# The finishing steps of three engines, written into both branches of a graph-network kernel

## What is computed

```
h = relu(layernorm(x))
for l in 1..3:                                    # RGCN, 8 relations, mean per relation
    h = relu(h @ root_l + b_l + sum_r mean_over_edges_of_relation_r((h @ W_l[r])[src], dst))
x = x + h
h = relu(layernorm(x))
h = h + segment_sum(h[src], dst)                  # GIN
h = relu(h @ W1 + b1) @ W2 + b2
h = (h - mean(h, axis=0)) * rsqrt(var(h, axis=0) + 1e-5) * gamma + beta
return x + h
```

## Time and profile before

| | |
|---|---|
| median of three runs | 1638.9 us (1638.22 to 1639.16) |
| the profiled execution's own time | 1638.72 us |
| its span, first to last instruction | 1636.7 us |
| mean granted TensorE clock | 0.669 of full |
| busy: TensorE (PE) | 1195.2 us, 73% |
| busy: GpSimd (POOL) | 1190.5 us, 73% |
| busy: VectorE (DVE) | 868.2 us, 53% |
| busy: ScalarE (ACT) | 643.9 us, 39% |

### The profile page before, as it was taken

How to read it: one execution, slowest core, us unless ns; L and a number is a source line. 1 busy time by engine, 2 the same in 40 slices (tenths; PEclk the granted TensorE clock), 3 DMA queues, 4 the chain that set the end, 5 groups by cost and what they waited for, 6 DMA issues and landing times. The chain is left out here.

```text
span 1636.7 us, 17097 instructions
## 1 busy us (share of the span) xinstructions
PE 1195.2 (73%) x4462; PEld 800.1 (49%) x4486; DVE 868.2 (53%) x3262; ACT 643.9 (39%) x1139; POOL 1190.5 (73%) x1257
## 2 busy tenths in 40 slices
PE   6989675757586878777868787875666666666786
PEld 3466444545455645454535354563544444444553
DVE  5778855555553387777787777742222221222214
ACT  5503200000000498888888888840012121212224
POOL 4777777777777777777777777767777777777770
PEclk9999655555555655657585757655576776767888
DMA  7934343434332322323232323322211221212211
GB/s 227 364 94 121 104 132 91 121 93 119 93 112 68 106 53 68 91 59 98 56 104 52 105 54 104 91 74 52 53 52 53 52 53 52 54 52 54 54 52 42
DMA packets 80864, 144.33 MB, mean 88 GB/s; under 512 B 24720, under 2 KB 38266, under 8 KB 80762
## 3 DMA queue, kind: packets, MB, share of 16 engines
q0 software_dynamic: 39936, 81.87, 19.9%
q1 hardware_dynamic: 40394, 60.67, 10.5%
q10 hardware_dynamic: 432, 0.64, 0.2%
HBM read 100.42 MB, written 42.67 MB: 87 GB/s over the span
## 5 line engine op out<-in xcount | busy, mean ns | idle before, releaser
L1154 POOL DMA_INDIRECT rows<-h_table,idx x1186 | 1125.4, 949 | 367.8 <-issue 367.8
L517 PE MATMUL ps_agg<-sel,rows 128*128 128x64 f32 (+13 forms) x2770 | 723.2, 378 | 401.7 <-DMA rows<-h_table,idx 390.6
L517 PEld LDWEIGHTS ps_agg<-sel,rows 128*128 128x128 f32 x2770 | 611.8, 282 | 696.5 <-DMA rows<-h_table,idx 532.9
L897 DVE TENSOR_SCALAR sel<-iota,early,norm 128x64 f32<-128x64 f32 x1186 | 357.0, 334 | 414.3 <-PE ps_agg L517 412.7
L992 DVE TENSOR_TENSOR early<-ps_a,early 128x300 f32 x416 | 197.9, 476 | 122.8 <-PE ps_a L584 115.6
L782 ACT ACTIVATE scratch<-scratch,ones 128x300 bf16<-128x300 f32 x416 | 222.7, 536 | 46.3 <-PE ps_a L584 39.1
L788 ACT ACTIVATE scratch<-iota,code_lo 128x300 f32<-128x300 f32 x416 | 226.5, 545 | 12.5
L491 PE MATMUL ps_h<-w_all,xT 128*128 128x512 f32 x300 | 196.2, 769 | 4.3 <-ACT stage L693 3.2
L875 DVE TENSOR_SCALAR_CACHE_REDUCE agg_s<-scratch,key_f 128x256 bf16<-128x256 int16 x416 | 192.9, 472 | 10.7 <-DMA scratch<-key_rows 9.4
L584 PE MATMUL ps_a<-scratch 128*128 128x300 bf16 x416 | 170.8, 411 | 1.5 <-DVE early L992 1.2
L981 DVE TENSOR_SCALAR scratch<-iota,code_lo 128x128 bf16<-128x128 f32 x416 | 143.8, 346 | 0.0
(11 more groups left out here) (150 smaller groups left out, 622.4 us busy)
## 6 DMA issues: line engine op xcount, KB each, us to landing
h_table<-stage SPq DMA_DIRECT2D x130, 256.0 KB, 2.4
rows<-h_table,idx POOLq DMA_INDIRECT x1186, 2.5
scratch<-key_rows SPq DMA_DIRECT2D x26, 544.0 KB, 4.1
h_table<-scratch SPq DMA_DIRECT2D x20, 256.0 KB, 6.1
x_rows<-in_x SPq DMA_DIRECT2D x6, 256.0 KB, 6.1
w_all<-in_W SPq DMA_DIRECT2D x3, 512.0 KB, 8.2
x_table<-early SPq DMA_DIRECT2D x6, 256.0 KB, 2.3
out<-early SPq DMA_DIRECT2D x6, 256.0 KB
```

The costliest lines, as they stand in the source:

```text
L517: mm = nc.tensor.matmul(sums_of(L, k)[:, at:at + width], rows[:, G % SLOTS, :], sel[:, G % SELS, in_window:in_window + width], start=False ...
L897: done = nc.vector.tensor_scalar(mine, here, dst, weight, ALU.is_equal, ALU.mult)
L1154: pool.indirect_dma_start(rows[:, slot, :], None, table, bass.IndirectOffsetOnAxis(ap=column, axis=0)).then_inc(landed, 16)
```

## The change

On each of ScalarE, VectorE and TensorE the finishing steps become a function `finish()`, which is called at the end of the fast branch and again at the end of the `Else`. The code behind both branches is gone. What the steps do, their order and their semaphores are the same. SyncE's and GpSimd's programs are as before. Cut to its core (TensorE's part has the same form as ScalarE's):

```diff
         @block.scalar
         def _(act):
+            def finish():
+                act.wait_ge(s_fin, 1)
+                nc.scalar.activation(small[:, 3:4], small[:, 2:3], ACT.Sqrt, bias=vecs[:, 7:8]).then_inc(s_fin_sd, 1)
+                act.wait_ge(s_fin, 5)
+                for q in range(GROUPS):
...
@@ -1266,6 +1277,7 @@
                         out_hid(act, q)
                     if q >= 1:
                         out_z(act, q - 1)
+                finish()
             with act.Else():
...
                     scalar_layer(act, L, False)
-            act.wait_ge(s_fin, 1)
-            nc.scalar.activation(small[:, 3:4], small[:, 2:3], ACT.Sqrt, bias=vecs[:, 7:8]).then_inc(s_fin_sd, 1)
-            act.wait_ge(s_fin, 5)
-            for q in range(GROUPS):
...
+                finish()
 
         @block.vector
         def _(dve):
+            def finish():
+                dve.wait_ge(s_fin_sd, 1)
+                nc.vector.reciprocal(small[:, 4:5], small[:, 3:4]).then_inc(s_fin, 1)
...
@@ -1430,6 +1451,7 @@
                 dve.wait_ge(s_bn, outs)
                 nc.vector.bn_aggr(small[:, 1:3], bn[:, 0:outs, :].rearrange("p b s -> p (b s)")).then_inc(s_fin, 1)
+                finish()
             with dve.Else():
...
                 nc.vector.bn_aggr(small[:, 1:3], bn[:, 0:SUMS[GIN], :].rearrange("p b s -> p (b s)")).then_inc(s_fin, 1)
-            dve.wait_ge(s_fin_sd, 1)
-            nc.vector.reciprocal(small[:, 4:5], small[:, 3:4]).then_inc(s_fin, 1)
...
+                finish()
```

More of the change, by code:

```diff
@@ L1187, in _ @@
         def _(act):
+            def finish():
[3 more added lines that the diff above has]
+                for q in range(GROUPS):
+                    b0, b1 = x_groups[q]
+                    if q >= 2:
+                        act.wait_ge(s_yturn, q - 1)
+                    nc.scalar.activation(y_turn[:, q % 2, 0:P * (b1 - b0)], xT[:, P * b0:P * b1], ACT.Identity,
+                                         bias=small[:, 6:7], scale=small[:, 5:6]).then_inc(s_y, 1)
             act.dma_start(dst_i, dst_t[:, 0:COLS]).then_inc(s_edges, 16)
@@ L1276, in _ @@
                     scalar_layer(act, L, False)
-            act.wait_ge(s_fin, 1)
-            nc.scalar.activation(small[:, 3:4], small[:, 2:3], ACT.Sqrt, bias=vecs[:, 7:8]).then_inc(s_fin_sd, 1)
-            act.wait_ge(s_fin, 5)
-            for q in range(GROUPS):
[L1281 to L1285, removed]
+                finish()
         @block.vector
         def _(dve):
+            def finish():
+                dve.wait_ge(s_fin_sd, 1)
+                nc.vector.reciprocal(small[:, 4:5], small[:, 3:4]).then_inc(s_fin, 1)
+                dve.wait_ge(s_fin, 2)
+                nc.vector.tensor_tensor(small[:, 5:6], small[:, 4:5], vecs[:, 5:6], ALU.mult).then_inc(s_fin, 1)
+                dve.wait_ge(s_fin, 3)
+                nc.vector.tensor_tensor(small[:, 7:8], small[:, 1:2], small[:, 5:6], ALU.mult).then_inc(s_fin, 1)
+                dve.wait_ge(s_fin, 4)
+                nc.vector.tensor_tensor(small[:, 6:7], vecs[:, 6:7], small[:, 7:8], ALU.subtract).then_inc(s_fin, 1)
+                dve.wait_ge(s_keep, SUMS[LAST_REL])
+                for q in range(GROUPS):
+                    b0, b1 = x_groups[q]
+                    dve.wait_ge(s_yturn, q + 1)
+                    nc.vector.tensor_tensor(y_rows[:, b0:b1, :].rearrange("p b f -> p (b f)"),
+                                            ps_agg[q % BANKS][:, 0:D * (b1 - b0)],
+                                            x_rows[:, b0:b1, :].rearrange("p b f -> p (b f)"), ALU.add).then_inc(s_yout, 1)
             nc.vector.memset(x_rows[:, LAST, :], 0.0).then_inc(s_const, 1)
@@ L1484, in _, with finish @@
                 nc.vector.bn_aggr(small[:, 1:3], bn[:, 0:SUMS[GIN], :].rearrange("p b s -> p (b s)")).then_inc(s_fin, 1)
-            dve.wait_ge(s_fin_sd, 1)
-            nc.vector.reciprocal(small[:, 4:5], small[:, 3:4]).then_inc(s_fin, 1)
[L1487 to L1499, removed]
+                finish()
         @block.tensor
         def _(pe):
+            def finish():
+                for q in range(GROUPS):
+                    b0, b1 = x_groups[q]
+                    pe.wait_ge(s_y, q + 1)
+                    if q >= BANKS:
+                        pe.wait_ge(s_yout, q - BANKS + 1)
+                    for b in range(b0, b1):
+                        at = P * (b - b0)
+                        mm = nc.tensor.transpose(ps_agg[q % BANKS][:, at:at + P], y_turn[:, q % 2, at:at + P], ident[:])
+                    mm.then_inc(s_yturn, 1)
             pe.wait_ge(s_pool_const, 1)
```

## The result

| | before | changed |
|---|---|---|
| median | 1638.74 us (22 runs, 1636.32 to 1641.86) | 1636.22 us (22 runs, 1633.8 to 1640.23) |
| ratio | | 0.9986, 95% interval 0.998 to 0.9993 |
| profiled execution: time, span | 1638.72, 1636.7 | 1638.27, 1636.4 |
| start of `bn_aggr` to end of span | 15.8 | 13.2 |

A forecast was written before the change was run, and what follows sets the result against it. GpSimd's gathers pace most of the kernel, untouched, so only the last 16 us matter, where two gaps go: 1638.72 - 2.38 = 1636.3 us, with the median 0.2 above, so 1636.5. Range 1635.3 to 1638.2 us.

The forecast's parts named there:

- The gaps are jumps: Between bn_aggr and first scaling activation: two 1.2 us gaps are ScalarE's and VectorE's jumps to far code; moving gains 2.38 us.
- TensorE's step gains nothing: Before the transposes: TensorE's jump was over at 1622.7, ahead of its wait's end at 1625.59, so moving it gives nothing.
- The groups keep their durations: Finishing groups: activations, 25 transposes, adds and stores keep their durations and move 2.38 us earlier.
- rival A: First transposes: TensorE keeps its full clock, shown by clock column 1.00; about 1635.5 us in full, chance 0.10.
- One fast group: First transposes at 2.4 GHz: one group at full clock brings the first store 0.6 us forward, giving 1635.9.
- in full: All transpose groups at the full clock: gain 3.4 us, 1635.5 us, DMA engines becoming the bound; chance 0.10.
- The jumps are covered: End of kernel: jumps and drains finish before SyncE's wait for stores ends at 1633.9; cost nothing, least slack 0.8 us, TensorE.
- The fetches beside the stores cost nothing: Store train at the end: code fetches sharing DMA engines cost 0, bounded at 1.27 us if holding up the last store.
- Rival C: End of kernel: fetches queue behind stores and jumps become the end; median 1639.3 us, or 1641.3 with a second packet; chance 0.05.
- The spread: Whole time: runs before spread by 0.9 us around their median; 0.4 us of spread went into the range's upper end.
- The sum: Whole kernel: 1638.72 less 2.38 gives 1636.3 us for the profiled execution; median forecast 1636.5 us, 0.15% less.
- B: Gaps behind bn_aggr: they are slow waits or first use of the square root, not jumps; gain 0, 1638.9 us; chance 0.05.

The follow-up runs named there:

- e4: Kernel before, with the slow branch on ScalarE, VectorE and TensorE cut to one instruction each; 1.48 us from bn_aggr to first scaling activation, 13.4 to the end.
- e1: Kernel before with ScalarE's finishing steps alone moved into both branches; 3.63 us from bn_aggr to first scaling activation (3.86 before), 15.7 to the end.
- e2: Kernel before with VectorE's finishing steps alone moved into both branches; 2.50 us from bn_aggr to first scaling activation (3.86 before), 14.5 to the end.
- e3: Kernel before with ScalarE's and VectorE's finishing steps moved, TensorE's left behind the branches; 1.49 us from bn_aggr to first scaling activation, 13.2 to the end.
- e9: The changed kernel again, unaltered, beside the kernel before on one chip; 1637.02 us (11 runs), ratio 0.9990 (0.9979 to 1.0001), 13.6 us from bn_aggr to the end.
- e5: Slow branch first, fast branch with finishing steps last on three engines, against the kernel before; 1633.2 us (6 runs), ratio 0.9968.
- e7: Fast branch last on three engines and last store split into 48 and 5 rows, against the kernel before; 1633.11 us (7 runs), ratio 0.9967.
- e10: Fast branch last on three engines and last store split, run again beside the changed kernel; 1634.29 us (5 runs), ratio 0.9963 to the kernel before.

## Why the prediction was right

1. *The gaps are jumps* (forecast 2.38 of gain by the head): right, and shown. The head went from 3.86 to 1.48. e4 shows that it is the distance of the jump, e1 and e2 that the two jumps run side by side.
2. *TensorE's step gains nothing*: right, by e3.
3. *The groups keep their durations*: nearly. The first group ran at 2.4 GHz, so the last add came 0.46 us sooner behind the first activation than before. That is rival A in part, and the sign that I had set for it, the clock column at 1.00 over the first transposes. One fast group I had priced at 0.6 and counted within the forecast; "in full" did not come about. The first transpose was fast in eight of the ten profiles in which its wait was cut to 3.6 us, and slow in e4 and e9, whose end is 0.3 to 0.6 longer than that of e5 and of the changed kernel's first profile.
4. *The jumps are covered*: right, with mis-sized terms. TensorE's jump beside the stores took 4.06 and 4.20 us, not 3.6 (its packet 1.59 and 1.68 us, not 1.27), and VectorE's next record came 3.5 us after its jump, not 3.0. The slack was 0.7 and 0.6 where I had 0.8.
5. *The fetches beside the stores cost nothing*: near enough in the changed kernel, too narrow as a bound. From the first store packet to the last it was 7.47 us before and 7.59 in the changed kernel, 0.1 more. But with the last store split it was 8.2 to 8.3 against 6.1 to 6.3 without jumps, 2.0 more, where I had bounded it at 1.27. The one packet from which I had argued that queues are served in turn, 0.55 us late at most, was too little to go by. Rival C has something to it, though SyncE's issue of the stores took part, which I had not thought of, and it did not come first in the changed kernel.
6. *The spread*: I had taken 0.4 us from three runs. The 22 runs of the kernel before spread over 5.5, those of the changed kernel over 6.4. The medians hold because there are many; the range, meant for the median, leaves out 13 of the changed kernel's 22 executions.
7. *The sum*: from `bn_aggr` to the end the gain was 2.7 us in the first pair of profiles, which is 2.38 of the head and 0.46 of the fast group, less 0.1 of a longer store train, and 2.0 to 2.2 in e9, where the transposes ran at 1.2 GHz from the first on. The forecast of the mechanism stands on these. That the median came within 0.3 us of the forecast is in part luck: the interval of the gain is some 2 us wide, and e9's runs gave 1.8.

B fell with e4. C did not come about in the changed kernel: SyncE was last at the barrier, in both of its profiles.

## What to carry to other kernels

Look in the chain of waits for "issue" pieces of a microsecond with no releaser, and in the queues' rows for a jump over a long branch just ahead: here, from the jump on, 2.6 to 3.7 us were lost to it with idle DMA engines, and on TensorE 4.1 to 5.5 beside stores. Put the work that everything waits for ahead of the jump on each engine of the chain, since moving one engine alone gained nothing (ScalarE) or half (VectorE). Better still here was to lay the branch that is taken last, so that nothing is jumped over at the end; with the last store split that is 0.33 to 0.37% below the kernel before. Look then at what the jump at the entry delays: here the delay happened to help, and in another kernel it may cost its 5 to 6 us.

## What was not expected

- TensorE's jump at the entry lasted 5.55 us in e5, 6.29 in e7 and 6.02 in e10, with the DMA engines busy with loads and tables, and none of the three kernels was slower for it: it broke up a burst of VectorE that held up GpSimd.
- An issue of a store by SyncE, otherwise 0.37 to 0.59 us, took up to 1.73 while TensorE fetched code.
- One store of 53 rows runs on a single DMA engine, 53 packets one behind the other. Split into 48 and 5 the end came 1.0 us sooner (e5 to e7). The page "DMA: Bandwidth & Descriptors" of the Trainium skill (section "Why a DMA increments its semaphore by 16 and not by 1") has the number of engines set by the largest divisor, up to 16, of the outermost size of the transfer, which is one for the 53 rows; the trace agrees with its DMA share of 0.07, one engine of 16.
